# One wide identity product and one block product of marks for four node tiles in a graph attention layer

## The reference, cut to what matters

```
h = x @ Wn + bn
for l in range(4):
    Q, K, V = h @ WQ[l] + bQ[l], h @ WK[l] + bK[l], h @ WV[l] + bV[l]
    attn = softmax over the edges into a node of (Q[dst] . K[src]) / sqrt(128)
    messages = segment_sum(attn * V[src], dst)
    h = layernorm(h + messages @ WO[l] + bO[l]) * ln_g[l] + ln_b[l]
out = h @ Wout + bout
```

## Time and profile before

| | |
|---|---|
| median of 3 runs | 7199.51 us (7189.98 to 7204.04) |
| the profiled execution | 7207.11 us |
| its span, first to last instruction | 7205.6 us |
| mean granted TensorE clock | 0.812 of 2.4 GHz |
| PE, DVE, ACT, POOL busy | 67%, 60%, 36%, 65% of the span |
| the four calls of `layer_turn` begin at | 1634.8, 2603.6, 3568.2, 4538.5 us |

### The profile page before, as it was taken

The page is one execution under the profiler, slowest core; times in us unless marked ns, Lnnn a source line. Parts: engine busy times, 40 slices in busy tenths (PEclk is TensorE's granted clock), DMA queues, the critical chain, the costliest instruction groups (busy, mean ns, idle before and its releaser), DMA issues. The chain is left out here.

```text
span 7205.6 us, 129339 instructions
## 1 busy us (share of the span) xinstructions
PE 4828.5 (67%) x28962; PEld 3965.0 (55%) x28963; DVE 4303.4 (60%) x13513; ACT 2629.9 (36%) x7476; POOL 4660.4 (65%) x4878
## 2 busy tenths in 40 slices
PE   5510477766777776777677777644555455997999
PEld 4310365655666664665556665522333334997998
DVE  7550366663666644666446666356777765766665
ACT  0200244433444443444334343314555543654111
POOL 1367577773777755777557777327777755776777
PEclk9555688887888887888778888676777776998999
DMA  5310233322333313333223332123333324333332
GB/s 185 98 36 0 70 89 91 90 78 54 91 90 91 88 40 95 88 90 89 58 75 89 93 88 83 30 92 98 105 105 105 105 77 113 95 97 82 97 95 84
DMA packets 404676, 615.62 MB, mean 85 GB/s; under 512 B 213466, under 2 KB 255993, under 8 KB 403884
## 3 DMA queue, kind: packets, MB, share of 16 engines
q0 software_dynamic: 169952, 363.29, 17.7%
q1 hardware_dynamic: 211126, 200.20, 9.7%
q10 hardware_dynamic: 23130, 47.29, 2.0%
HBM read 528.32 MB, written 82.09 MB: 85 GB/s over the span
## 5 line engine op out<-in xcount | busy, mean ns | idle before, releaser
L1973 POOL DMA_INDIRECT rows<-table_d,meta x2432 | 2307.0, 949 | 886.7 <-issue 726.1
L2037 PE MATMUL ps_total<-weighted_rows,ident 128*128 128x129 f32 (+1 forms) x6464 | 1393.4, 371 | 604.9 <-ACT weighted_rows L2197 489.3
L2037 PEld LDWEIGHTS ps_total<-weighted_rows,ident 128*128 128x128 f32 x6464 | 1137.8, 223 | 866.6 <-issue 680.0
L2373 DVE SCALAR_TENSOR_TENSOR prod<-rows,q_rows 128x129 f32<-128x129 f32 x2432 | 689.4, 293 | 633.1 <-issue 386.7
L1973 POOL DMA_INDIRECT rows<-pairs_d,meta x800 | 776.8, 971 | 257.8 <-issue 242.8
L2073 PE MATMUL dense_sums<-x_rows,dense_power_t 128*128 128x129 f32 x3528 | 598.6, 322 | 448.2 <-DVE dense_rows L2264 433.6
L2073 PEld LDWEIGHTS dense_sums<-x_rows,dense_power_t 128*128 128x128 f32 x3528 | 538.4, 232 | 487.6 <-issue 487.6
L2141 ACT ACTIVATE weighted_rows<-rows,power 128x129 f32<-128x129 f32 x2432 | 729.5, 389 | 4.9
L2159 ACT COPY dense_power_t<-dense_turned 128x512 f32<-128x512 f32 x504 | 265.1, 526 | 1031.3 <-PE dense_turned L2064 1025.3
L2197 ACT ACTIVATE weighted_rows<-once_weighted,of_relation 128x136 f32<-128x136 f32 x1600 | 484.9, 393 | 195.5 <-DVE once_weighted L2433 193.2
L2254 DVE CUSTOM_DVE_ANT_0 dense_masked<-dense_scores,dense_masked,dense_least 128x896 f32<-128x896 f32 x252 | 289.1, 1147 | 412.8 <-PE dense_scores L2055 291.6
(11 more groups left out here) (700 smaller groups left out, 9141.0 us busy)
## 6 DMA issues: line engine op xcount, KB each, us to landing
dense_masked<-dense_masks_d SPq DMA_DIRECT2D x252, 448.0 KB
rows<-table_d,meta POOLq DMA_INDIRECT x2432, 2.5
dense_masks_d<-unmasked ACTq DMA_DIRECT2D x9, 3136.0 KB
src_store<-near_window_d SPq DMA_DIRECT2D x50, 384.0 KB, 3.7
near_window<-near_window_d SPq DMA_DIRECT2D x48, 384.0 KB, 3.6
rows<-pairs_d,meta POOLq DMA_INDIRECT x800, 2.8
tile_rows<-table_d,tile_halves POOLq DMA_INDIRECT x441, 2.6
tile_rows<-made_d,tile_halves POOLq DMA_INDIRECT x441, 2.5
```

Of the source, the lines that this page charges most:

```text
L1973: pool.indirect_dma_start(rows[q][:, j, 0:width], None, table_d, bass.IndirectOffsetOnAxis(meta[q][:, j, number:number + 1], 0)).then_inc( ...
L2037: mm = pe.matmul(total[:, q, ds(part, 1), 0:W].rearrange("p a w -> p (a w)"), k.ident[:], wide[:, j % WS, :], start=False, stop=True, skip ...
L2373: own(dve.scalar_tensor_tensor(prod[:, j % 2, :], rows[q][:, j, :], -1.0, query, ALU.mult, ALU.mult, accum_out=score[:, j, :]))
```

## The change

The old rows of the four tiles of a group go into `sum_ps` with one product of 512 columns in place of four of 128, and the bias rows likewise: the marks of tile j of a group now lie in rows 32j and 32j + 1, and `add4` is a matrix of blocks which holds the two bias rows in rows 32j and 32j + 1 of block j alone, with zeros elsewhere. A single product over 98 rows (`BROWS`) then adds the biases of four tiles. For this, POOL first clears `add4` and the columns of the marks; SP waits for that and issues nine DMAs in place of one; PE multiplies by `bv` spread over 98 columns, so that the product bV @ WO stands in 98 rows; DVE copies four rows of it in place of one, behind the same clearing; and bO is loaded by SP in `layer_turn` and no longer by ACT in `edge_pass`.

```diff
-FETCHED = {False: 10, True: 8}
+FETCHED = {False: 9, True: 7}
+BROWS = 32 * (GB - 1) + 2
...
-    act.dma_start(k.add2[1:2], I["L0_gnn_bO"][ds(l, 1)]).then_inc(m["fetched"], 16)
...
+        add4 = buf(nc, s, "lt_add", [P, GB, P])
...
-                sp.dma_start(k.marks[0:2], k.marks_d.rearrange("r (t p) -> r t p", p=P)).then_inc(m["marked"], 16)
+                sp.wait_ge(m["unmarked"], 2)
+                of_group = k.marks_d[:, 0:(NGB - 1) * GB * P].rearrange("r (g j p) -> r j g p", j=GB, p=P)
+                for j in range(GB):
+                    sp.dma_start(k.marks[32 * j:32 * j + 2, 0:NGB - 1, :], of_group[:, j]).then_inc(m["marked"], 16)
+                    sp.dma_start(add4[32 * j + 1:32 * j + 2, j, :], I["L0_gnn_bO"][ds(l, 1)]).then_inc(m["marked"], 16)
+                sp.dma_start(k.marks[0:2, NGB - 1, :], k.marks_d[:, (NGB - 1) * GB * P:NPAD]).then_inc(m["marked"], 16)
...
-                pe.matmul(w_ps[0:1, 3, :], k.bv[:], k.raw["WO"][:], start=True, stop=True).then_inc(m["raw_ps"], 1)
-                pe.wait_ge(m["raw"], 2)
+                pe.matmul(w_ps[0:BROWS, 3, :], k.bv[:].to_broadcast([P, BROWS]), k.raw["WO"][:], start=True, stop=True).then_inc(m["raw_ps"], 1)
+                pe.wait_ge(m["raw"], 1)
...
-                            pe.wait_ge(m["marked"], 16)
+                            pe.wait_ge(m["marked"], 16 * (2 * GB + 1))
+                            pe.wait_ge(m["raw"], 2)
...
-                        for j, t in enumerate(group_tiles(g)):
-                            o = sum_ps[g % 2][:, j, :]
-                            pe.matmul(o, k.ident[:], k.h[:, t, :], start=True, stop=False)
-                            pe.matmul(o, k.marks[0:2, t, :], k.add2[0:2], start=False, stop=False)
-                            mm = pe.matmul(o, at[g % 2][:, j, :], wvo[:], start=False, stop=True)
+                        n = len(group_tiles(g))
+                        pe.matmul(sum_ps[g % 2][:, 0:n, :], k.ident[:], k.h[:, g * GB:g * GB + n, :], start=True, stop=False,
+                                  skip_group_check=True)
+                        pe.matmul(sum_ps[g % 2][:, 0:n, :], k.marks[0:BROWS, g, :], add4[0:BROWS, 0:n, :], start=False, stop=False,
+                                  skip_group_check=True)
+                        for j in range(n):
+                            mm = pe.matmul(sum_ps[g % 2][:, j, :], at[g % 2][:, j, :], wvo[:], start=False, stop=True, skip_group_check=True)
...
-                dve.tensor_copy(k.add2[0:1], w_ps[0:1, 3, :]).then_inc(m["raw"], 1)
+                for j in range(GB - 1):
+                    if j == 0:
+                        dve.wait_ge(m["unmarked"], 2)
+                    own(dve.tensor_copy(add4[32 * j:32 * j + 1, j, :], w_ps[32 * j:32 * j + 1, 3, :]))
+                own.wait()
+                dve.tensor_copy(add4[BROWS - 2:BROWS - 1, GB - 1, :], w_ps[BROWS - 2:BROWS - 1, 3, :]).then_inc(m["raw"], 1)
...
+                    pool.memset(add4[:], 0.0).then_inc(m["unmarked"], 1)
+                    pool.memset(k.marks[:, 0:NGB, :], 0.0).then_inc(m["unmarked"], 1)
```

More of the change, by code:

```diff
@@ L2721, in fetch_layer, with layer_turn @@
     act.dma_start(k.bk[:], column("bK", l + 1), allow_slow_non_contiguous=True).then_inc(m["fetched"], 16)
-def layer_turn(nc, k, last, x_d):
+def layer_turn(nc, k, I, l, last):
+    x_d = I["x"]
     made = ["WV"] if last else ["WV", "WQ", "WK"]
@@ L2730, in layer_turn @@
                                "summed_ps", "stat", "rooted", "scale", "normed", "stored", "rows_ps", "rows", "out_ps", "out_taken",
-                               "scattered", "marked"] + [f"kept{g}" for g in range(NGB if last else 0)])
+                               "scattered", "marked", "unmarked"] + [f"kept{g}" for g in range(NGB if last else 0)])
         wt = {n: buf(nc, s, f"wt_{n}", [P, P + 1]) for n in made}
         wvo = buf(nc, s, "wvo", [P, P])
+        add4 = buf(nc, s, "lt_add", [P, GB, P])
         wz = buf(nc, s, "wz", [P, P + 1])
@@ L3380, in _ @@
                 dve.memset(k.acc[:, :, 0:P + 1], 0.0)
-                dve.memset(k.add2[:], 0.0)
                 dve.memset(k.x[:], 0.0)
@@ L3580, in gnn_kernel @@
             k.bv = buf(nc, s, "bv", [P, 1])
-            k.add2 = buf(nc, s, "add2", [P, P])
             k.gb = buf(nc, s, "ln_g", [P, P])
@@ L3586, in gnn_kernel @@
                 edge_pass(nc, k, "attend", k.table_d, NPAD, P, *listed[0:3], dn.sched, fetch=(I, l, False), sort=(so, l), dn=dn)
-                layer_turn(nc, k, False, I["x"])
+                layer_turn(nc, k, I, l, False)
             edge_pass(nc, k, "attend", k.table_d, NPAD, P, *listed[0:3], dn.sched, fetch=(I, k.layers - 1, True), sort=(so, k.layers - 1), dn=dn)
-            layer_turn(nc, k, True, I["x"])
+            layer_turn(nc, k, I, k.layers - 1, True)
         place_rest(nc, k, so, L.sched, chunks)
```

## The result

The changed kernel takes 7108.18 us (median of 4 runs, 7094.96 to 7111.43) against 7200.27 us (median of 4, 7189.98 to 7204.04): a ratio of 0.9871, 95% interval 0.9854 to 0.9888, so 92 us less. It was measured again later beside other runs of the kernel before: 7101.23 against 7187.92, ratio 0.9873 (0.9854 to 0.9892), 87 us less. The forecast was 7098, with a range of 7082 to 7152.

What follows compares the result with a forecast made beforehand. The prediction took PE to set the pace of `layer_turn`. Gains of 50.8 (scatters), 16.8 (first scatters), 33 (turn 4) and 1 us (bO's load) make 102, from 7199.5 to 7098 us, range 7082 to 7152.

Steps and rivals of the forecast that it cites:

- What bounds the kernel before: In `layer_turn`, PE sets the pace of a turn: 5.99 us a group at 2.4 GHz, against POOL's 5.09.
- The sums of a group: PE's sums of a group fall from 4.22 to 2.57 us at 2.4 GHz, with no gaps around 98 rows.
- What is late next: POOL's scatters become the limit of turns 1 to 3, one every 1.27 us: 50.8 us gained.
- The clock: PE's clock rises 6 us after the sums of group 0 begin in a turn.
- Rival A: PE's clock rises no sooner than now, taking 54 us off the gain: 7151 us, chance 0.16.
- rival B: PE's clock stays at 1.2 GHz for the whole turn: 49 us slower, 7249 us, chance 0.02.
- The start of a turn: POOL's clearing and SP's nine DMAs delay the first sums of each turn by 2.4 us, bounds 1.5 and 5.
- first scatters: In turns 1 to 3, entry to first scatter shortens by 5.6 us each, from 20.5 to 14.9: 16.8 us gained.
- Rival D: Marks come 8 us late at a turn's start, through slow issue and landing: 22 us lost, 7120 us, chance 0.08.
- Turn 4: In turn 4, where nothing is scattered, a group takes 4.6 us (bounds 4.34 and 5.0): 33 us gained.
- Rival C: ACT and DVE set 5.5 us a group in all turns: 23 us lost, 7121 us, chance 0.06.
- The sum: Over the whole kernel, 50.8 + 16.8 + 33 + 1 = 102 us gained, from 7199.5 to 7098 us.

Runs made afterwards that it cites:

- experiment 2: The changed kernel with its identity and marks products cut to 128 columns, marks still over 98 rows: 7100.79 us, ratio 0.9862; measured again, 7101.13 us, ratio 0.9875.
- experiment 3: The kernel before with one wide identity product, then four 2-row marks products in a row, then the four turned sums; nothing cleared: 7117.32 us, ratio 0.9886.
- experiment 4: The changed kernel with two more products of 512 columns of zeros per group: 7150.52 us, ratio 0.9930.
- experiment 5: The changed kernel with one more product of 256 columns of zeros per group: 7106.48 us, ratio 0.9889.
- experiment 6: The changed kernel without the scatters of the odd tiles in turns 1 to 3: 7057.97 us, ratio 0.9817.
- experiment 8: The changed kernel with POOL clearing 3328 more columns ahead of the marks: 7113.78 us, ratio 0.9897.
- experiment 1: The kernel before with only the identity products of a group made one of 512 columns, marks still two rows per tile: 7196.25 us, ratio 0.9993.

## Why the prediction was right, step by step

**What bounds the kernel before** held. PE's gaps set the pace of a turn: with them gone (experiment 2), or made fewer (experiment 3), the turns shrink, and even with products of zeros in place of the gaps, so that a group takes as long as before, half of the gain is left (experiment 4).

**The sums of a group**: 2.57 us forecast, 2.61 measured. Of the two bounds on the product over 98 rows, none and 0.42 us, it is none. So the choice between them, which no row could settle, was right. Experiment 3 adds that the price falls on the change of rows and not on the small product. The rule of the Trainium skill that was weighed there (TensorEngine Tiling, Tiling Modes: a change of tiling mode drains the array) agrees with all three: 0.2 us on each side of one product of two rows, 0.4 to 0.5 us in all for the two changes around four in a row, nothing at 98 rows.

**What is late next**: POOL, as said. It has no wait after its first scatter, more PE work costs nothing there (experiment 5), fewer scatters give over 40 us (experiment 6). The term was 5.3 too large, since I took every distance from the earlier trace rows as 1.27, and some scatters of up to 1.45 us bring the mean distance to 1.31.

**The clock** rose, and sooner than taken: 4.8, 3.7, 2.3 and 2.5 us after the sums of group 0 began in the four turns. I had taken 6. Rival A (no sooner than before) and rival B (not at all) are out by the traces of all four turns. Rival B also had its cause wrong, since PE waits for POOL nowhere in a turn, and its differences add up to 53 us, not 49. The price of 0.41 us per us at half clock was one for the changed kernel, and no run held that kernel at half clock. The kernel before shows 0.45: its turns with 28.8, 38.3 and 50.5 us of half clock have their last scatter at 99.8, 104.1 and 109.6 us. In experiment 4, 155 us less of it shortened the four turns of the profiled execution by 63 us (0.41 each), with groups that cost PE 0.11 us more; the medians give 51.

**The start of a turn**: a delay of 2.4 us was forecast, 0.2 us came in turn 1 and none in the others. The step that failed is the distance of SP's DMAs, taken as 0.46 us from sixteen others; these take 0.33. They also land in 1.8 us and not in 2.1 to 2.4. The chain starts its clearing 0.2 us after the turn and is done as PE arrives. Experiment 8 shows that it is done just then: 2.87 us more of clearing are 2.78 us of waiting. So the gain of the first scatters was 26.3 and not 16.8: 2.2 to 2.4 us in each turn for this, and some 1 us for the clock, which rose 1.2, 2.3 and 3.7 us sooner than taken. Rival D (marks 8 us late) is out.

**Turn 4**: 4.60 us per group forecast and measured. The gain was 36.9, 3.9 more, 2.4 of it again the delay that did not come, the rest the earlier clock. That a group takes 4.60 where PE needs 4.38 fits the handing over between ACT and DVE that was allowed for; no run took that apart. Rival C (5.5 us a group) is out, and with it the warning of the Trainium skill that it stood beside (TensorEngine Tiling, Performance Considerations, PSUM bottleneck; the page has it for a TensorE four times as fast, and here a group of PE's work shrank from 5.99 to 4.38 us): the copies of ACT and DVE keep up with PE within 0.22 us a group.

**The sum**: 102 forecast, 112 between the profiled executions, 92 and 87 between the medians (100 for the same products cut narrow in experiment 2). Against the profiled pair the terms err by +9.5 (first scatters), -5.3 (scatters), +3.9 (turn 4) and +2.4 (the rest): they partly cancel. The rest of the way to 7108 is that the profiled execution of before lay high among its runs. So the mechanism was right in each of its steps but the start of a turn, while that 7098 and 7108 lie 10 us apart is in part luck. The kernel before spreads over 40 us (7175.8 to 7216.9 in one group), the changed one over 3 to 16. Its half clock lasts between 29 and 51 us from turn to turn, and one that also differs from run to run would explain that spread. Only profiled executions show the clock by stretch, but the mean granted clock of each run points the same way: in that group the four shortest runs (7175.8 to 7184.3) have 0.811 to 0.813 and the longest (7216.9) has 0.809. That is a hint and no proof.

**What stays open**: why a few scatters take 1.45 us instead of 0.97 (the kernel before had none over 1.18); what it is in the gaps that keeps the clock down, beyond that it stays down with them and rises without them; from how many rows between 2 and 98 on a product has no gap, since no run tried one; and how much of the 3.4 us outside the turns is bO's load leaving ACT's queue, since no run did that part alone.

## What to carry to other kernels

Look for short products over few rows between products over many, at the idle time before weight loads: the rows of PE's busy time had no hole, and yet two fifths of the sums' time (0.42 of 1.06 us a tile) were gaps, and the granted clock stood at half for tens of microseconds. Put such products side by side, or give them rows of zeros so that they use about as many rows as their neighbours (here 98 beside 128); the zeros cost no time in the product. Before crediting a change with two parts, run each alone: the part with the wide product gave nothing, and reordering alone gave over four fifths (84 of 100 us). When PE stops being the limit, look at once for what follows, here a queue of scatters that is worth another 40 us or more.

## What the runs showed of the hardware

- A float32 product over 2 rows between products over 128 costs 0.2 us more on each side (0.84 us for it and its successor against 0.43, all at 2.4 GHz); over 98 rows it costs nothing extra (0.22 us each, experiment 2). Four of two rows in a run cost 1.09 us together (experiment 3).
- PE at 100% busy with such gaps stayed at 1.2 GHz for 29 to 51 us from its first sum; without them it was at 2.4 GHz 2.3 to 4.8 us after it. With the gaps left in but wide products between some of them (experiment 1), the clock went up and down within a turn while PE was 100% busy. At equal work per group the higher clock is worth 51 us in 7200 (experiment 4).
- SP's small DMAs start every 0.33 us here and every 0.46 us elsewhere in the same kernel, and the last landed 1.8 us after its issue (experiment 8).
- POOL's indirect scatters, once nothing holds them up, start every 1.27 us for the most part; single ones take up to 1.5 us themselves (0.97 is usual).
